# Early-fusion network on one core: GpSimd takes the clamp and the sum of the hyperbolic distance

## What is computed

```
inner = einsum(q, k) - tq * tk^T          # tq = sqrt(1/curv + |q|^2), tk likewise
arg = maximum(-curv * inner, 1.0 + 1e-07)
dis = sqrt(1/curv) * arccosh(arg)
scores = 1 / (eps + dis) + causal_bias
out = softmax(scores) @ v
```

## Time and profile before

| | us |
|---|---|
| median of 3 runs | 5960.48 |
| lowest, highest | 5957.14, 5983.22 |
| the profiled execution | 5973.35 |
| its span | 5971.3 |
| TensorE busy | 4632.2 (78%) |
| VectorE busy | 3844.7 (64%) |
| ScalarE busy | 2507.9 (42%) |
| GpSimd busy | 597.5 (10%) |

### The profile page before, as it was taken

One profiled execution on the slowest core, in us unless ns is written; L12 is line 12 of the kernel. 1 busy time (PEld: TensorE's weight loads), 2 busy tenths in 40 slices (PEclk: granted clock), 3 DMA queues, 4 the chain that ended last, 5 costly groups with the idle time before them and its releaser, 6 DMA issues. The chain is left out here.

```text
span 5971.3 us, 101861 instructions
## 1 busy us (share of the span) xinstructions
PE 4632.2 (78%) x27583; PEld 3020.9 (51%) x27583; DVE 3844.7 (64%) x9327; ACT 2507.9 (42%) x5760; POOL 597.5 (10%) x928
## 2 busy tenths in 40 slices
PE   6999978850029888587787786777799899789888
PEld 5667657640015555355555554555455555444444
DVE  3444433348878878777777665555677777477776
ACT  1222224347533333377777774222366666400000
POOL 0000000000000000100000000111111111122221
PEclk9999989975569989777777777888799999899999
DMA  2111113348974444332222222555433333211110
GB/s 65 52 54 52 50 53 144 144 169 253 355 274 125 127 130 123 87 75 69 69 69 69 71 72 69 157 154 154 105 93 85 88 94 91 77 45 46 49 50 27
DMA packets 379998, 617.03 MB, mean 103 GB/s; under 512 B 43190, under 2 KB 310004, under 8 KB 379892
## 3 DMA queue, kind: packets, MB, share of 16 engines
q1 hardware_dynamic: 367572, 614.35, 35.1%
q0 software_dynamic: 12320, 1.40, 0.2%
HBM read 345.02 MB, written 269.21 MB: 103 GB/s over the span
## 5 line engine op out<-in xcount | busy, mean ns | idle before, releaser
L1645 DVE TENSOR_REDUCE e_neg<-ps 91x1 f32<-91x273 f32 x1536 | 571.9, 427 | 137.4 <-PE ps L1466 130.0
L1578 ACT ACTIVATE e_probT<-ps 91x273 f32<-91x273 f32 x1536 | 491.7, 393 | 292.9 <-PE ps L1466 292.2
L1193 PE MATMUL ps<-k_downT,f_o 128*91 128x256 f32 x1152 | 260.1, 385 | 453.6 <-DVE f_o L1101 453.4
L2320 PE MATMUL ps<-m_we,m_xT 128*128 128x512 f32 x1104 | 521.6, 621 | 0.0
L1193 PEld LDWEIGHTS ps<-k_downT,f_o 128*91 128x91 f32 x1152 | 183.0, 161 | 522.4 <-issue 454.6
L1464 PE MATMUL ps<-c_mask_kq,c_identb 91*91 91x91 bf16 x1536 | 325.8, 243 | 104.4 <-ACT g_probT L1578 79.4
L1466 PE MATMUL ps<-e_k,e_q 96*91 96x273 bf16 x1536 | 344.0, 307 | 64.9 <-DMA e_k<-s_parts 28.8
L2254 DVE SCALAR_TENSOR_TENSOR m_acc<-ps,m_weight,m_acc 128x256 f32<-128x256 f32 x552 | 261.7, 481 | 173.6 <-PE ps L2320 163.7
L1466 PE MATMUL ps<-g_q,g_k 102*91 102x273 bf16 (+5 forms) x1536 | 331.0, 296 | 49.1 <-DVEq L1651 48.5
L2320 PEld LDWEIGHTS ps<-m_we,m_xT 128*128 128x128 f32 x1104 | 211.4, 198 | 223.3 <-issue 208.9
L1466 PE MATMUL ps<-e_q,e_k 128*91 128x273 bf16 x1536 | 286.7, 291 | 38.3 <-DMA e_q<-e_shift 36.4
(11 more groups left out here) (303 smaller groups left out, 10057.6 us busy)
## 6 DMA issues: line engine op xcount, KB each, us to landing
s_gate<-b_gu SPq DMA_DIRECT2D x32, 819.0 KB
s_up<-b_gu SPq DMA_DIRECT2D x32, 819.0 KB
c_g<-s_gate SPq DMA_DIRECT2D x32, 819.0 KB, 7.0
s_gated<-c_g SPq DMA_DIRECT2D x32, 819.0 KB
d_g<-s_gated SPq DMA_DIRECT2D x32, 819.0 KB, 10.4
d_u<-s_up SPq DMA_DIRECT2D x32, 819.0 KB
s_o<-d_o SPq DMA_DIRECT2D x32, 819.0 KB
f_o<-s_o SPq DMA_DIRECT2D x32, 819.0 KB
```

The source lines that it names most:

```text
L1193: last = nc.tensor.matmul(ps[0:R, t // 2, (t % 2) * D:(t % 2 + 1) * D], o[:, u, k, t * R:(t + 1) * R], downT[:, k, :], start=(k == 0), sto ...
L1578: nc.scalar.activation(probT[0:R, p % 8, b, :], src, ACT.Exp, scale=float(HD) ** 0.5 if kinds[h] == COS else 1.0)\
L1645: last = nc.vector.tensor_reduce(neg[:, u, t, h:h + 1], src, AX.X, ALU.max, negate=True)
L2320: last = nc.tensor.matmul(ps[0:R, EBANK[m % 4], :], xT[:, u, k, t * R:(t + 1) * R], we[:, k, 2 * p:2 * p + 2, :].rearrange("p e d -> p (e ...
```

## The change

The clamp L1664 and the sum L1675 go from VectorE's program to GpSimd's, in the same steps. GpSimd gives the semaphores `z` and `wc`. In a step GpSimd does the clamp of a head whose look is there, waiting for `w` and `looked`, or the sum of a head whose look was two steps earlier, waiting for `root`; of two heads the lower number comes first, so the sum of head a - 1 stands ahead of the clamp of head a. After each wait stands an event instruction (`pool.sem_inc(passed, 1)`). VectorE keeps its waits for `z` and `wc` ahead of L1669, which now name GpSimd's work.

```diff
+            for x in ("z", "wc") if n_hyp else ():
+                S[x].give(pool)
+
             def step(when, p, n, u, i):
+                for a, h in enumerate(HYPS):
+                    if (when, p) == place(look_step[h]):
+                        y = max(uses[(h, "raw", b)] for b in range(UNITS))
+                        pool.wait_ge(S["w"].sem, S["w"].at(n, a + 1))
+                        pool.sem_inc(passed, 1)
+                        pool.wait_ge(S["looked"].sem, S["looked"].at(n, y + 1))
+                        pool.sem_inc(passed, 1)
+                        nc.gpsimd.tensor_scalar(hw[:, u, a], hw[:, u, a], 2.0 ** -23, None, ALU.max)\
+                            .then_inc(S["wc"].sem, 1)
+                    if (when, p) == place(look_step[h] + SUM):
+                        pool.wait_ge(S["root"].sem, S["root"].at(n, a + 1))
+                        pool.sem_inc(passed, 1)
+                        nc.gpsimd.tensor_tensor(hw[:, u, a], hw[:, u, a], hu[:, a], ALU.add).then_inc(S["z"].sem, 1)
...
-            for x in ("looked", "rest", "lo", "rec", "out") + (("top", "w", "wc", "hu", "z", "hneg", "shifted") if n_hyp else ()):
+            for x in ("looked", "rest", "lo", "rec", "out") + (("top", "w", "hu", "hneg", "shifted") if n_hyp else ()):
...
-
-                        dve.wait_ge(S["w"].sem, S["w"].at(n, a + 1))
-                        dve.wait_ge(S["looked"].sem, S["looked"].at(n, y + 1))
-                        nc.vector.tensor_scalar(hw[:, u, a], hw[:, u, a], 2.0 ** -23, None, ALU.max)\
-                            .then_inc(S["wc"].sem, 1)
                         dve.wait_ge(S["z"].sem, S["z"].at(n, a + 1 - n_hyp))
                         dve.wait_ge(S["wc"].sem, S["wc"].at(n, a + 1))
...
-                for a, h in enumerate(HYPS):
-                    if (when, p) == place(look_step[h] + SUM):
-                        dve.wait_ge(S["root"].sem, S["root"].at(n, a + 1))
-                        nc.vector.tensor_tensor(hw[:, u, a], hw[:, u, a], hu[:, a], ALU.add).then_inc(S["z"].sem, 1)
```

## The result

The changed kernel takes 6171.4 us (median of 4, 6161.2 to 6176.4), the kernel before beside it 5971.9: ratio 1.0331, interval 1.0295 to 1.0367. That is 3.3% slower, some 197 us, where 41 us (0.7%) and a range up to 6045 had been forecast. The direction was right, the size was wrong by a factor of nearly five. The profiled execution has a span of 6159.5 us, 188.2 more than before.

A forecast was written before the change was run, and what follows sets the result against it. VectorE's order up to the fourth square was taken to bound each batch. Clamp waits of 4 x 0.64 less freed sums of 2 x 0.64 gave 1.27 us a batch, times 32 = 41 us: median 6001 us, range 5940 to 6045.

The forecast's parts named there:

- What bounds the kernel: Causal core: VectorE's four hyperbolic looks up to the fourth L1669 set a 37.0 us batch, then about 10 us of ScalarE.
- ScalarE is full behind it: Behind the fourth L1669: ScalarE busy almost without a break up to the copy L1604, 6.57 of 7 us.
- The freed sums: L1675 on VectorE: only the first two sums count, 2 x 0.64 = 1.29 us a batch; the last two nothing.
- The clamp's length: The clamp on GpSimd: 1.10 us, from rows of 4 and 36 elements; bounds 0.62 and 1.34.
- the upper bound, an addition with two inputs: The clamp on GpSimd: 2.10 ns an element from two-input addition rows, so 1.34 us at most.
- The hand-overs: Between VectorE and GpSimd around the clamp: 0.08 over and 0.03 back, rounded up to 0.13 us a head.
- The held small instruction: Rival, chance 0.23: L1653 on VectorE held by GpSimd's first sum, 0.65 us more a batch, 6022 us.
- The part of a batch behind the fourth L1669 keeps its length.: From the fourth square to the batch's end: no change in time.
- The range: 5940 to 6045 us, leaving out the faster case and the far end of the held-instruction rival.
- its highest case: Held L1653 with a clamp of 1.34 us as well: 2.9 us a batch, 92 us, 6053 us.

The follow-up runs named there:

- half clamp: The changed kernel with GpSimd clamping only the first 274 of 549 columns, the rest left unclamped: 6038.3 us, ratio 1.0097 to the kernel before.
- short token: The kernel before, but each square L1669 also waits for GpSimd to fill a 91x3 scratch tile after the clamp: 6013.1 us, ratio 1.0052.
- folded: The kernel before without a clamp instruction: L1653 and L1658 take the maximum, the logarithm takes the minus 1 as bias: 5894.1 us, ratio 0.9861.
- add_tile: The changed kernel with GpSimd adding a tile filled with the floor (tensor_tensor) in the clamp's place: 6125.6 us, ratio 1.0247 to the kernel before.
- add_floor: The changed kernel with GpSimd's tensor_scalar adding the floor instead of taking the maximum: 6157.0 us, ratio 1.0304 to the kernel before.
- square_later: The changed kernel with the square L1669 two steps after its look, root and sum a step later: 6041.6 us, ratio 1.0111 to the kernel before.
- first two sums: The kernel before with only the sums of the first two hyperbolic heads on GpSimd: 5991.8 us, ratio 1.0025.
- added work: The changed kernel with every look of the first four plain heads done twice on TensorE: 6144.7 us, ratio 1.0271 to the kernel before.

## Why the prediction went wrong, point by point

- *What bounds the kernel.* Right for the stretch up to the fourth square, from both sides: waits longer (changed, half clamp, short token) and clamp gone (folded). That ScalarE is full behind it holds in many batches and not in all: where TensorE's clock is low in its middle, ScalarE waits for TensorE there.
- *The freed sums.* 1.29 us a batch was forecast for the stretches from sq to w; 1.25 was measured. That the last two are free was right too (at most 17 us by their run's interval). But the first two alone made no kernel faster: the part behind the fourth sq got 0.95 us longer.
- *The clamp's length* is the term that was mis-sized most: 1.10 taken, 1.58 measured, 4 x 0.48 = 1.9 us a batch, 61 us. It does not explain the miss alone: with 1.58 the prediction's own sum gives 4 x (1.58 - 0.46) - 1.29 = 3.2 us a batch, 102 us, half of what was measured. The step that failed is the slope from rows of 4 and 36 elements, and with it the upper bound, an addition with two inputs: another form is no bound, as the add_tile and add_floor kernels show. The rule of the Trainium skill that was weighed ("GPSIMD Engine Reference", section 4.1, one input at roughly line rate) is contradicted by these rows: they have 2.51 ns an element, where one element a cycle of that page's 1.2 GHz would be, as an estimate, 0.83.
- *The hand-overs.* 0.13 taken, 0.30 measured, 4 x 0.17 = 0.7 us a batch, 22 us.
- *The held small instruction.* I left it out for its size, though the row of the same form spoke for it. It is held: 0.62 us for the second head, 0.66 a batch over all, 21 us. The rule on the shared ports (the Trainium skill, "SBUF — State Buffer", section Who interferes with whom) agrees with this, and with the squares of square_later.
- *"The part of a batch behind the fourth L1669 keeps its length."* Wrong: plus 1.03 us, 33 us. The same work took longer where TensorE's granted clock was low while ScalarE waited for its scores. The prediction put this term at nothing without looking at the clock. What lowers the clock is not shown: longer waits ahead agree with four kernels and not with the one of the first two sums, and the one attempt to lift it by added work moved the part by 0.4 us only.
- The forecast and the four terms that it missed: 1.27 + 1.9 + 0.7 + 0.66 + 1.03 = 5.6 us a batch, against 5.58 measured.
- *The range* ended at 6045 since its highest case combined a clamp of 1.34 with the held instruction, and had neither the clock nor the hand-overs as an open term.

## What to carry over

An instruction that is moved off a full engine, but which the next instruction of that engine needs at once, frees nothing: price it as the gap from the producer's end to the consumer's start on the other engine (here 1.88 for 0.59 us), and look first for a way to fold it into a neighbour. Where no row of the size exists on the engine, a slope from a few elements is only a guess (here 1.56 ns for 2.51), and another form of instruction is no bound. And when a change moves TensorE's work in time, leave a term for its clock in the part that follows: here it was minus 0.5 to plus 2.3 us a batch.

## What the runs showed of the hardware

- GpSimd's tensor_scalar with a constant, f32, 91 partitions: 886 ns for 274 columns and 1577 for 549 with the maximum, 1594 with the addition; its tensor_tensor addition 1346 for 549. Against a tile of one value that does not change the addition took 1.34 us for the first two heads and 1.15 for the last two; why they differ was not looked into.
- VectorE to GpSimd and back costs 0.30 us in two hand-overs in this stage, without the work (changed kernel and short token).
- A VectorE instruction of three elements is held by GpSimd's two-input addition until that ends (0.82 to 1.07 us instead of 0.22 for the second head), and the squares with two inputs in SBUF reach 1.79 us instead of 0.73.
- With the same work for TensorE and ScalarE, the part of a batch behind the fourth square took 16.0 us in a batch where TensorE's granted clock was 1.00 in its middle, 17.0 in one where it was 0.57 there for 4 us, and about 20 in batches with a mean near 0.6. What sets the clock from batch to batch stays open.
